# Rows for the next projections turned by VectorE and through memory instead of by TensorE, and the first six weight loads issued at once

## The chip, the core and the metric

The kernel runs on one core of a Trainium2 chip. The core has TensorE (PE in the profile, for matrix products), VectorE (DVE), ScalarE (ACT), GpSimd (POOL) and SyncE (SP), which issues the transfers. Each engine takes its instructions in order, and semaphores join the queues. The metric is the device time of one execution in microseconds, lower is better; every kernel is run several times and the median is given.

## The reference

A block of attention and an MLP over x of 16 x 256 rows of width 256, with a layer norm before and after each part and a residual around it:

```
x = x + layernorm(attention(layernorm(x)))     # 16 heads of 128, causal, biases on q, k, v, o
x = x + layernorm(mlp(layernorm(x)))           # 2048 wide, out = (gelu(gate) * up) @ Wd.T

scores = where(causal, q @ k.T / sqrt(128), -1e5);  attn = softmax(scores)
W = LUT[4-bit codes] * scales[block of 32]     # gate, up and down weights of the MLP
```

All of it is fp32. The layer norms have no weights: (x - mean) / sqrt(var + 1e-5).

## The kernel before

**Precision.** TensorE multiplies in fp32r, so each operand is split into a high part (`_hi`, rounded by a copy on ScalarE) and a low part (`_lo`, the difference, on VectorE or GpSimd), and a product is three matmuls, hi x hi, lo x hi and hi x lo (`three`, lines 700 to 702).

**Tiling.** The 4096 rows are eight chunks (`NCH`) of 512 rows: two sequences, four tiles of 128 rows (`TT`). The width of 256 is two tiles for the contraction (`KT`), and these take every second column, kt, kt+2, and so on. Attention is 128 steps, n = 16 c + j for chunk c and head j; the MLP after it is eight chunks of sixteen tiles of its hidden width. `xnT` holds the normalised rows of a chunk, turned (width on the partitions, 512 rows along), in a high and a low part; all projections of a chunk read it.

**One step of attention.** `step_plan(n)` is written out by hand: projections q and k of head n+1, T(n) (VectorE turns the probabilities of head n in blocks of 32 x 32 into `turned`), out(n-3), z(n-2), pT(n-1), scores(n+1). In steps with n % 4 = 1 the four value tiles of the next four heads, v0 to v3, follow. In step 14 of a chunk, before, the plan also holds xT 0 and xT 1: TensorE transposes the next chunk's normalised rows out of `stream`, four 128 x 128 transposes for each (line 719), ScalarE and VectorE evict them into `xnT_hi` and `xnT_lo`. Projections, z and xT take the three PSUM banks `fbank` in turns, and a bank is free once the low part of what it held is written. Scores use three banks `ubank`.

**VectorE's order** is that of the plan with z moved behind the scores. Then follow, at the place "sum", the reciprocals of the softmax sums (line 901) and what `extra(c, j, "sum")` adds, and after v3, at "end", what `extra(c, j, "end")` adds. Two tables say what is added: `X1_AT`, the parts of the norm and residual of the attention's output of the chunk before (`finish_x1`), and `NEXT_AT`, the parts of the next chunk's layer norm (`norm_next_x`: 0 and 1 statistics, 2 their aggregates, 3 and 4 standardising). GpSimd takes the square roots in between, in steps `X1_ROOTS` and `NEXT_ROOTS`. `spread` unpacks 4-bit weights of the MLP beside all this.

**The probabilities' way through memory.** A turn in blocks of 32 leaves the blocks in the wrong partitions. In each step SyncE stores `turned` to a scratch in memory (`send`, line 488) and, once stored, loads it back in four pieces, each to its 32 partitions (`fetch`, line 498), into `back`, whence ScalarE takes pT. SyncE's queue (`load_program`) holds per step: send, the loads of weights (`load_pair`, chunk 0 only), fetch, store and load of the MLP's unpacked weights, and then, by j, a half of the next x (j = 3, 5), a half of x1's store (11, 13) or a half of the residual's x (15 and the next 1). `load_pair` uses two buffers (`raw`, `RAW` = 2) in turns: pair n waits until pair n-2 is split.

**The MLP.** `mlp_plan(c, j)`: gate and up products of tile j+2, then the down product of tile j. `finish_y` (j < 6) and `norm_next_y` (j = 7 to 10) add the norms on VectorE (`between`). At j = 13, before, the next chunk's rows are transposed on TensorE into `gbank` and `hbank` and evicted into `xnT`.

## Time and profile before

| | |
|---|---|
| median of 3 runs | 1584.81 us (1583.91 to 1586.49) |
| profiled execution | 1591.08 us, span 1588.4 us, granted clock 0.998 |
| TensorE busy | 1561.3 us, 98% |
| VectorE | 1061.5 us, 67% |
| ScalarE | 974.1 us, 61% |
| GpSimd | 712.5 us, 45% |
| transposes of rows, TensorE | 64 in attention, 56 in the MLP |
| traffic | 167.69 MB, mean 106 GB/s |

The span is the time on the engines and the profiled execution's own time is a little longer. Busy shares are averages over the whole span. A matmul of 512 columns is listed with 0.39 us, but a new one starts every 0.23 us, since they are pipelined; lengths of stretches are therefore read as the distance of two starts. I cut attention at the first scores matmul of each step (line 724).

### The profile page before, as it was taken

To read this page: it belongs to the slowest core of one execution; us is meant where nothing else is said; L and a number is where in the kernel's file an instruction comes from. 1 tells how busy PE (TensorE), PEld (TensorE's weight loads), DVE (VectorE), ACT (ScalarE), POOL (GpSimd) and SP (SyncE) were. 2 spreads that over 40 slices of the span, in tenths; PEclk is the share of its full clock that TensorE was granted. 3 is DMA by queue.
4 is the path that set the end of the run, shared out by engine and by line. 5 is a ranking of instruction groups with operands and counts; after the bars stand their busy time and mean duration, and the time that the engine had idled before them with its cause. 6 is when DMAs were issued, how large, how long until landed. Compare 5 with 4: busy or idle time off the path is not lost.

```text
span 1588.4 us, 28430 instructions
## 1 busy us (share of the span) xinstructions
PE 1561.3 (98%) x9600; PEld 1397.9 (88%) x9600; DVE 1061.5 (67%) x3074; ACT 974.1 (61%) x2433; POOL 712.5 (45%) x1069
## 2 busy tenths in 40 slices
PE   7999999999999999999999999999999999999998
PEld 5889898988998899889899989898888888888887
DVE  4656677677677777777767766666656565565665
ACT  5887677667776676767776767644444444444443
POOL 4674454545554455444554544333333333333333
PEclk9999999999999999999999999999999999999999
DMA  4554434443444344444443454471000011000000
GB/s 118 178 174 122 140 116 139 149 138 124 143 148 138 123 144 131 140 130 131 149 143 117 142 163 136 155 278 41 27 14 27 14 32 36 14 28 14 27 14 27
DMA packets 157440, 167.69 MB, mean 106 GB/s; under 512 B 15856, under 2 KB 130672, under 8 KB 157296
## 3 DMA queue, kind: packets, MB, share of 16 engines
q1 hardware_dynamic: 157296, 165.89, 32.9%
q8 instruction: 76, 1.25, 0.3%
q14 instruction: 68, 0.56, 0.1%
HBM read 94.53 MB, written 71.30 MB: 104 GB/s over the span
## 4 chain that ended last, share of the span: by engine, by line
PE 79%; DMA 6%; ACT 6%; DVE 5%; SPq 3%; issue 1%; POOL 1%; DVEq 0%; POOLq 0%
PE fbank L700 13%; PE fbank L701 13%; PE fbank L702 13%; PE obank L702 6%; PE obank L701 6%; PE obank L700 6%; PE ubank L700 5%; PE ubank L702 5%; PE ubank L701 5%; DMA turned_scratch<-turned 3%; PE ubank L724 3%; PE fbank L802 2%; DMA back<-turned_scratch 2%; SPq L498 2%; ACT probs L597 1%
## 5 line engine op out<-in xcount | busy, mean ns | idle before, releaser
L700 PE MATMUL fbank<-xnT_hi,wqk_hi 128*128 128x512 f32 x768 | 302.9, 394 | 3.7 <-POOL wqk_lo L1215 2.7
L701 PE MATMUL fbank<-xnT_lo,wqk_hi 128*128 128x512 f32 x768 | 301.3, 392 | 0.0
L702 PE MATMUL fbank<-xnT_hi,wqk_lo 128*128 128x512 f32 x768 | 300.7, 392 | 0.0
L1246 POOL TENSOR_TENSOR pT_lo<-back,pT_hi 128x512 fp32r<-128x512 f32 x128 | 166.1, 1298 | 274.3 <-ACT pT_hi L662 274.3
L608 ACT ACTIVATE w_raw<-fbank 128x512 f32<-128x512 f32 x128 | 76.5, 598 | 254.3 <-PE fbank L702 254.3
L1208 POOL TENSOR_SCALAR probs<-probs,rsum 128x128 f32<-128x128 f32 (+1 forms) x512 | 209.2, 428 | 20.7 <-DVE rsum L901 17.7
L702 PEld LDWEIGHTS fbank<-xnT_hi,wqk_lo 128*128 128x128 f32 x768 | 145.1, 189 | 31.8
L893 DVE CUSTOM_DVE_ANT_0 probs<-ubank,mask 128x128 f32<-128x128 f32 (+1 forms) x512 | 154.9, 355 | 26.4 <-PE ubank L702 26.1
L700 PEld LDWEIGHTS fbank<-xnT_hi,wqk_hi 128*128 128x128 f32 x768 | 145.2, 189 | 27.6 <-issue 2.9
L701 PEld LDWEIGHTS fbank<-xnT_lo,wqk_hi 128*128 128x128 f32 x768 | 145.3, 189 | 22.5
L982 DVE SCALAR_TENSOR_TENSOR w_raw<-w_raw,fbank 128x512 f32<-128x512 f32 x128 | 88.0, 687 | 104.0 <-ACT w_raw L608 102.2
L1226 POOL TENSOR_TENSOR kT_lo<-probs,kT_hi 128x512 fp32r<-128x512 f32 x64 | 83.1, 1298 | 160.4 <-ACT kT_hi L617 160.4
L988 DVE SCALAR_TENSOR_TENSOR probs<-w_raw,fbank 128x512 f32<-128x512 f32 x128 | 88.1, 688 | 97.8 <-ACT w_raw L612 97.8
L1226 POOL TENSOR_TENSOR v_lo<-probs,v_hi 128x512 fp32r<-128x512 f32 x64 | 82.8, 1294 | 153.4 <-ACT v_hi L617 153.4
L578 ACT ACTIVATE zT_hi<-fbank,bias_v 128x512 fp32r<-128x512 f32 x128 | 87.4, 683 | 104.0 <-PE fbank L802 104.0
L700 PE MATMUL obank<-wo_hi,zT_hi 128*128 128x256 f32 x512 | 143.5, 280 | 0.0
L702 PE MATMUL obank<-wo_hi,zT_lo 128*128 128x256 f32 x512 | 143.4, 280 | 0.0
L701 PE MATMUL obank<-wo_lo,zT_hi 128*128 128x256 f32 x512 | 142.9, 279 | 0.0
L880 DVE SCALAR_TENSOR_TENSOR kT_lo<-fbank,bias_k,kT_hi 128x512 fp32r<-128x512 f32 x128 | 95.8, 749 | 54.4 <-ACT k_early L589 54.0
L1051 DVE STREAM_TRANSPOSE turned<-probs 128x384 f32<-128x384 f32 x256 | 131.5, 552 | 0.0
L597 ACT ACTIVATE probs<-probs,nmax 128x256 f32<-128x256 f32 x256 | 126.8, 495 | 0.0
L595 ACT ACTIVATE probs<-probs,nmax 128x128 f32<-128x128 f32 x256 | 100.7, 393 | 18.2 <-DVE nmax L893 15.6
(124 smaller groups left out, 4566.1 us busy)
## 6 DMA issues: line engine op xcount, KB each, us to landing
turned_scratch<-turned SPq DMA_DIRECT2D x128, 384.0 KB, 2.6
back<-turned_scratch SPq DMA_DIRECT2D x512, 96.0 KB, 2.2
w_raw<-in_w_pairs SPq DMA_DIRECT2D x32, 256.0 KB, 3.3
w_hi_scratch<-w_hi SPq DMA_DIRECT2D x48, 128.0 KB, 2.0
w_lo_scratch<-w SPq DMA_DIRECT2D x48, 128.0 KB, 2.0
x_res<-in_x SPq DMA_DIRECT2D x16, 256.0 KB, 2.9
wqk_hi<-w_hi_scratch SPq DMA_DIRECT2D x16, 256.0 KB, 4.6
wqk_lo<-w_lo_scratch SPq DMA_DIRECT2D x16, 256.0 KB, 5.0
```

The costliest lines, as they stand in the source:

```text
L595: act.activation(pr[:, 0:P], pr[:, 0:P], ACT.Exp, bias=nmax[:, 0:1], scale=-1.0, accum_out=sums[:, 0:1])
L597: act.activation(pr[:, P:384], pr[:, P:384], ACT.Exp, bias=nmax[:, 1:2], scale=-1.0, accum_out=sums[:, 1:2]).then_inc(s.exp, 1)
L700: nc.tensor.matmul(out, a[0], b[0], start=start, stop=False, skip_group_check=skip)
L701: nc.tensor.matmul(out, a[0], b[1], start=False, stop=False, skip_group_check=skip)
L702: return nc.tensor.matmul(out, a[1], b[0], start=False, stop=stop, skip_group_check=skip)
L880: ins = dve.scalar_tensor_tensor(dst, bank, bias, hi.bitcast(F32), ALU.add, ALU.subtract)
L893: last = dve.tensor_tensor_reduce(out=pr[:, lo:hi], in0=bank[:, lo:hi], in1=mask, scale=-SCALE, scalar=3.0e38, op0=ALU.add, op1=ALU.min, a ...
L988: after(dve.scalar_tensor_tensor(act_v, mem.th[j % 2], 1.0, mem.gbank[slot(n)][:], ALU.add, ALU.mult))
L1051: dve.transpose(mem.turned[:, :, :, b, :].rearrange("p k u j -> p u k j"), mem.probs[b].rearrange("p (u k j) -> p u k j", u=3, k=4)).then_ ...
L1208: last = pool.tensor_scalar(pr[:, lo:hi], pr[:, lo:hi], mem.rsum[i][:, at:at + 1], 1.0, ALU.mult, ALU.mult)
L1226: pool.tensor_tensor(lo, mem.act_v[j % 2], hi.bitcast(F32), ALU.subtract).then_inc(s.iT_lo, 1)
L1246: pool.tensor_tensor(lo[:].rearrange("p u b (a j) -> p (u b) a j", j=32), mem.back[m % 2][:, :, 0:2].rearrange("p a u b j -> p (u b) a j") ...
```

## The change

**Attention.** The plan's xT entries go. In step 9, at "sum", VectorE turns the four standardised row tiles of the next chunk in blocks of 32 x 32 (`turn_rows`); the source is read with a stride of two columns, since a contraction tile takes every second column. SyncE stores the 512 KB to a new scratch and loads them back in four pieces into `x_in`, behind step 9's fetch. In step 14, behind k, an entry "rows" stands for two copies on ScalarE (`rows_hi`) and two differences on VectorE (`rows_lo`) into `xnT`. The next chunk's layer norm moves forward, statistics to step 1, roots to step 3, standardising to step 5 (in place, in `x_in`); the loads of x that feed it move to step 15 of the chunk before, both halves. The residual's loads go to steps 1 and 3, and two parts of `finish_x1` from step 9 to steps 10 and 12.

**MLP.** The next rows are normalised at j = 7 and 8 and turned at j = 8, go through memory likewise, and are split at j = 12, into `xnT` or, in every second chunk, into `zT` and `pT`, which the MLP has free.

**Weights.** `FIRST_PAIRS` is 6: six loads go at once, into `raw`, `x_res` and `back`; every later one comes a step sooner.

```diff
-FIRST_PAIRS = 4
+FIRST_PAIRS = 6
-X1_ROOTS, NEXT_ROOTS = 6, 13
+X1_ROOTS, NEXT_ROOTS = 6, 3
 def step_plan(n):
     plan = [("q", n + 1), ("k", n + 1), ("T", n)]
     if n % HEADS == HEADS - 2:
-        plan += [("xT", 0)]
+        plan.insert(2, ("rows", n // HEADS + 1))
     if n > 2:
         plan += [("out", n - 3)]
-    if n % HEADS == HEADS - 2:
-        plan += [("xT", 1)]
 def mlp_plan(c, j):
-    if j == NT - 3:
-        return ahead + ([("xT", 0)] if c < NCH - 1 else []) + [("down", j)]
+    if j == NT - 4 and c < NCH - 1:
+        return ahead + [("rows", c + 1), ("down", j)]
 def load_program(...):
     def load_pair(n):
-        if n >= RAW:
-            sp.wait_ge(s.w_split, n - RAW + 1)
-        sp.dma_start(mem.raw[:, n % RAW], w_pairs[n]).then_inc(s.w[n % RAW], 16)
+        if n < FIRST_PAIRS:
+            sp.dma_start(mem.raw_of(n), w_pairs[n]).then_inc(s.first_w[n], 16)
+        else:
+            sp.wait_ge(s.w_split, n - RAW + 1 if n >= FIRST_PAIRS + RAW else RAW)
+            sp.dma_start(mem.raw_of(n), w_pairs[n]).then_inc(s.w[n % RAW], 16)
+    def send_rows(n):
+        sp.wait_ge(s.rows_turned, 2 * n + 2)
+        if n:
+            sp.wait_ge(s.rows_back, 64 * n)
+        sp.dma_start(rows_v.rearrange("a i k c -> (a i) k c"),
+                     mem.turned_at(n).rearrange("p k t r i -> p k (t r i)")
+                     ).then_inc(s.rows_sent, 16)
+    def fetch_rows(n):
+        sp.wait_ge(s.rows_sent, 16 * (n + 1))
+        for k in range(4):
+            sp.dma_start(mem.rows_back[32 * k:32 * k + 32].rearrange("p a t r i -> p a (t r i)"),
+                         rows_v[:, :, k].rearrange("a i c -> i a c")).then_inc(s.rows_back, 16)
         fetch(n)
+        if j == 9:
+            send_rows(c)
+            fetch_rows(c)
-        if j in (3, 5):
-            next_x(c, (j - 3) // 2)
-        elif c and j in (11, 13):
+        if c and j in (11, 13):
             store_x1(c, (j - 11) // 2)
         elif j == 15:
-            load_res(c, 0)
-            if c == NCH - 1:
-                load_res(c, 1)
-        elif c and j == 1:
-            load_res(c - 1, 1)
+            for i in range(2):
+                if c < NCH - 1:
+                    next_x(c + 1, i)
+                else:
+                    load_res(c, i)
+        elif c and j in (1, 3):
+            load_res(c - 1, (j - 1) // 2)
 def scalar_program(...):
+    def rows_hi(n, dst):
+        act.wait_ge(s.rows_back, 64 * (n + 1))
+        for kt in range(KT):
+            act.activation(dst[0][kt].rearrange("p (t a i) -> p t a i", a=4, i=BLK),
+                           mem.rows_back[:, :, :, kt, :].rearrange("p a t i -> p t a i"),
+                           ACT.Copy).then_inc(s.rows_hi, 1)
 def vector_program(...):
+    def turn_rows(n, t):
+        for i in (t, t + 1):
+            last = dve.transpose(mem.turned_at(n)[:, :, i].rearrange("p k r i -> p r k i"),
+                                 x_in[:, i, :].rearrange("p (k j r) -> p r k j", r=KT, j=BLK))
+        last.then_inc(s.rows_turned, 1)
+    def rows_lo(n, dst):
+        for kt in range(KT):
+            dve.wait_ge(s.rows_hi, KT * n + kt + 1)
+            dve.tensor_tensor(dst[1][kt].rearrange("p (t a i) -> p t a i", a=4, i=BLK),
+                              mem.rows_back[:, :, :, kt, :].rearrange("p a t i -> p t a i"),
+                              dst[0][kt].bitcast(F32).rearrange("p (t a i) -> p t a i", a=4, i=BLK),
+                              ALU.subtract).then_inc(s.rows_lo, 1)
-    X1_AT = {(5, "end"): (0, 1, 2), (9, "end"): (3, 4, 5, 6)}
-    NEXT_AT = {(10, "sum"): (0,), (12, "sum"): (1, 2), (13, "end"): (3, 4)}
+    X1_AT = {(5, "end"): (0, 1, 2), (9, "end"): (3, 4), (10, "sum"): (5,), (12, "sum"): (6,)}
+    NEXT_AT = {(1, "end"): (0, 1, 2), (5, "end"): (3, 4), (9, "sum"): (5, 6)}
     def between(c, j):
-        elif 7 <= j < 11 and c < NCH - 1:
-            norm_next_y(j - 7, c)
+        elif j == 7 and c < NCH - 1:
+            for part in range(2):
+                norm_next_y(part, c)
+        elif j == 8 and c < NCH - 1:
+            for part in range(2, 5):
+                norm_next_y(part, c)
```

VectorE's queue in step 9 of chunk 3, from the reciprocals on, before:

```order
913 L901 RECIPROCAL rsum<-sums 128x2 x2
914 L878 TENSOR_TENSOR v_lo<-fbank,v_hi 128x512 x2
915 L916 TENSOR_SCALAR stream<-stream,mv,rstd 128x256 x4
916 L932 TENSOR_TENSOR stream<-stream,x_res 128x512 x2
917 L956 TENSOR_SCALAR spread<-words 128x128
918 L958 SCALAR_TENSOR_TENSOR spread<-words,spread 128x128
```

and after (`w_raw<-x_in` are the turned rows, written to the weights' former buffer):

```order
918 L943 RECIPROCAL rsum<-sums 128x2 x2
919 L964 STREAM_TRANSPOSE w_raw<-x_in 128x2x4x32 x4
920 L920 TENSOR_TENSOR v_lo<-fbank,v_hi 128x512 x2
921 L958 TENSOR_SCALAR stream<-stream,mv,rstd 128x256 x4
922 L1014 TENSOR_SCALAR spread<-words 128x128
923 L1016 SCALAR_TENSOR_TENSOR spread<-words,spread 128x128
```

Four turns of 128 x 256 stand ahead of the value tiles' low parts, and the two residual sums (L932 before) have left.

VectorE's queue where step 14 of chunk 3 goes over into step 15, before:

```order
989 L880 SCALAR_TENSOR_TENSOR qT_lo<-fbank,bias_q,qT_hi 128x256
990 L880 SCALAR_TENSOR_TENSOR kT_lo<-fbank,bias_k,kT_hi 128x512
991 L1051 STREAM_TRANSPOSE turned<-probs 128x3x4x32 x2
992 L878 TENSOR_TENSOR xnT_lo<-fbank,xnT_hi 128x512 x2
993 L893 ISA probs,nmax<-ubank,mask 128x128
```

and after:

```order
992 L922 SCALAR_TENSOR_TENSOR qT_lo<-fbank,bias_q,qT_hi 128x256
993 L922 SCALAR_TENSOR_TENSOR kT_lo<-fbank,bias_k,kT_hi 128x512
994 L971 TENSOR_TENSOR xnT_lo<-x_in,xnT_hi 128x512 x2
995 L1109 STREAM_TRANSPOSE turned<-probs 128x3x4x32 x2
996 L935 ISA probs,nmax<-ubank,mask 128x128
```

The rows' low parts have moved ahead of the turn of the probabilities, and their source is `x_in` instead of a PSUM bank.

SyncE's queue in steps 15 and 16 (chunk 3 into 4), before:

```order
262 L498 DMA back<-turned_scratch 32x4x192 x4
263 L468 DMA x_res<-in_x 128x2x256
264 L488 DMA turned_scratch<-turned 128x768
265 L498 DMA back<-turned_scratch 32x4x192 x4
266 L480 DMA w_hi_scratch<-w_hi 128x256
```

and after:

```order
267 L527 DMA back<-turned_scratch 32x4x192 x4
268 L486 DMA x_in<-in_x 128x2x256 x2
269 L517 DMA turned_scratch<-turned 128x768
270 L527 DMA back<-turned_scratch 32x4x192 x4
271 L509 DMA w_hi_scratch<-w_hi 128x256
```

Two loads of the next x now stand between the fetch of one step's probabilities and the send of the next's, where one load of the residual stood.

VectorE's queue in step 1 of chunk 0, before:

```order
35 L901 RECIPROCAL rsum<-sums 128x2 [waits exp_ready] x2
36 L880 SCALAR_TENSOR_TENSOR qT_lo<-fbank,bias_q,qT_hi 128x256 [waits full_hi]
37 L880 SCALAR_TENSOR_TENSOR kT_lo<-fbank,bias_k,kT_hi 128x512 [waits full_hi]
38 L878 TENSOR_TENSOR v_lo<-fbank,v_hi 128x512 [waits full_hi]
39 L1051 STREAM_TRANSPOSE turned<-probs 128x3x4x32 [waits turned_stored,probs_ready]
40 L1051 STREAM_TRANSPOSE turned<-probs 128x3x4x32 [waits probs_ready]
```

and after:

```order
37 L922 SCALAR_TENSOR_TENSOR kT_lo<-fbank,bias_k,kT_hi 128x512 [waits full_hi]
38 L920 TENSOR_TENSOR v_lo<-fbank,v_hi 128x512 [waits full_hi]
39 L948 BN_STATS stats<-x_in 128x6 [waits x_loaded]
40 L948 BN_STATS stats<-x_in 128x6
41 L948 BN_STATS stats<-x_in 128x6 [waits x_loaded,dve_chain]
42 L948 BN_STATS stats<-x_in 128x6
43 L953 BN_AGGR mv<-stats 128x2 [waits dve_chain]
44 L953 BN_AGGR mv<-stats 128x2 x3
45 L1109 STREAM_TRANSPOSE turned<-probs 128x3x4x32 [waits turned_stored,probs_ready]
46 L1109 STREAM_TRANSPOSE turned<-probs 128x3x4x32 [waits probs_ready]
```

The statistics of the next rows stand behind the last value tile and ahead of the turn of the probabilities.

## Rows read from the trace of the kernel before

**Rows 1.** the head of the page: span, then busy time of each engine

```profile
span 1588.4 us, 28430 instructions
PE 1561.3 (98%) x9600; PEld 1397.9 (88%) x9600; DVE 1061.5 (67%) x3074; ACT 974.1 (61%) x2433; POOL 712.5 (45%) x1069
```

**Rows 2.** waits of TensorE: waiter, releaser, total us, times, longest

```profile
PE ubank L724 <- DVE kT_lo L880: 4.4, 8, 1.4
PE fbank L700 <- POOL wqk_lo L1215: 2.7, 1, 2.7
PE fbank L700 <- DVE v_lo L878: 1.8, 4, 0.6
```

**Rows 3.** window of step 9, chunk 3: stretch, length, busy by engine, clock, DMA

```profile
476.47:488.36 11.89, 11.89 (x70) 10.47 (x69) 8.87 (x28) 7.25 (x18) 3.94 (x8) 1.00 0.27 87
```

**Rows 4.** windows, scores of step 14 to those of step 15, their sum

```profile
sum 107.23, PE 104.78 PEld 91.33 DVE 70.20 ACT 66.97 POOL 38.17; mean PE 13.10 PEld 11.42 DVE 8.78 ACT 8.37 POOL 4.77
```

**Rows 5.** windows of step 1, chunks 1 to 7: the first, and the sum

```profile
157.25:170.08 12.83, 12.23 (x70) 10.40 (x69) 6.87 (x23) 7.31 (x19) 4.81 (x9) 1.00 0.37 111
sum 85.51, PE 84.29 PEld 73.20 DVE 47.12 ACT 52.04 POOL 31.86; mean PE 12.04 PEld 10.46 DVE 6.73 ACT 7.43 POOL 4.55
```

**Rows 6.** windows in the MLP: a quiet tile, and a chunk's sixteen

```profile
1300.25:1304.39 4.14, 4.14 (x27) 3.66 (x26) 2.06 (x4) 1.75 (x3) 1.29 (x1) 1.00 0.00 0
1239.88:1307.13 67.25, 67.25 (x394) 59.58 (x393) 41.32 (x77) 30.14 (x52) 23.06 (x20) 1.00 0.08 24
```

**Rows 7.** timeline of VectorE, step 9, chunk 3: start, length, what, idle before

```profile
475.86 1.03 DVE L1051 STREAM_TRANSPOSE turned<-probs 128x384 f32<-128x384 f32 x2
...
479.82 0.17 DVE L901 RECIPROCAL rsum<-sums 128x2 f32<-128x2 f32 x1 [0.62 <-ACT probs L597]
480.31 0.69 DVE L878 TENSOR_TENSOR v_lo<-fbank,v_hi 128x512 fp32r<-128x512 f32 x1 [0.32 <-ACT v_hi L577]
...
483.16 1.50 DVE L916 TENSOR_SCALAR stream<-stream,mv,rstd 128x256 f32<-128x256 f32 x4
```

**Rows 8.** timeline of TensorE, the fourth value tile of step 9, chunk 3

```profile
481.72 0.39 PE L700 MATMUL fbank<-wv_hi,xnT_hi 128*128 128x512 f32 x1
```

**Rows 9.** timelines of VectorE and TensorE, step 9, chunk 0

```profile
98.10 0.69 DVE L878 TENSOR_TENSOR v_lo<-fbank,v_hi 128x512 fp32r<-128x512 f32 x1 [0.32 <-ACT v_hi L577]
98.85 0.50 PE L700 MATMUL fbank<-wv_hi,xnT_hi 128*128 128x512 f32 x1 [0.54 <-DVE v_lo L878]
```

**Rows 10.** timelines of VectorE and TensorE, step 5, chunk 3

```profile
451.90 1.53 DVE L906 BATCH_NORM_STATS2 stats<-stream 128x6 f32<-128x256 f32 x4
453.47 0.38 DVE L911 BATCH_NORM_AGGREGATE mv<-stats 128x2 f32<-128x6 f32 x4
...
455.83 0.75 DVE L880 SCALAR_TENSOR_TENSOR kT_lo<-fbank,bias_k,kT_hi 128x512 fp32r<-128x512 f32 x1 [0.43 <-ACT k_early L589]
457.11 0.39 PE L724 MATMUL ubank<-k_early,q_early 128*128 128x128 f32 x2
```

**Rows 11.** timelines of VectorE and ScalarE, step 14 into 15, chunk 3

```profile
522.01 1.29 DVE L878 TENSOR_TENSOR xnT_lo<-fbank,xnT_hi 128x512 fp32r<-128x512 f32 x2 [0.32 <-ACT xnT_hi L577]
523.88 0.40 ACT L595 ACTIVATE probs<-probs,nmax 128x128 f32<-128x128 f32 x1 [0.21 <-DVE nmax L893]
```

**Rows 12.** timeline of SyncE, steps 0 and 1 of chunks 1 and 4

```profile
150.23 0.42 SPq L468 DMA_DIRECT2D x_res<-in_x  x1
151.25 0.33 SPq L488 DMA_DIRECT2D turned_scratch<-turned  x1
156.16 1.75 SPq L498 DMA_DIRECT2D back<-turned_scratch  x4
...
536.20 0.34 SPq L488 DMA_DIRECT2D turned_scratch<-turned  x1
538.80 1.74 SPq L498 DMA_DIRECT2D back<-turned_scratch  x4
```

**Rows 13.** timeline of TensorE, the scores of step 3

```profile
39.57 0.49 PE L724 MATMUL ubank<-k_early,q_early 128*128 128x128 f32 x2 [1.44 <-DVE kT_lo L880]
```

More of the change, by code:

```diff
@@ L657, in scalar_program @@
                 full(count, mem.zT[0][:], bank, mem.bias_v[:, h:h + 1]).then_inc(s.hi, 1)
-            else:
-                full(count, mem.xnT[0][:, m, :], bank).then_inc(s.hi, 1)
+        elif kind == "rows":
+            rows_hi(m - 1, mem.rows[0])
         elif kind == "pT":
@@ L715, in project @@
         last.then_inc(s.full, 1)
-    def transpose_x(src, kt, bank):
-        for t in range(TT):
-            last = nc.tensor.transpose(bank[:, t * P:(t + 1) * P], src[:, t, kt:D:KT], mem.ident[:])
-        return last
     def scores(u, i, b):
@@ L1043, in vector_program @@
                     extra(c, j, "sum")
-            else:
-                full(count, mem.xnT[1][:, m, :], mem.xnT[0][:, m, :], bank)
+        elif kind == "rows":
+            rows_lo(m - 1, mem.rows[0])
         elif kind == "T":
```

138 lines of the change are left out of this document (77 added, 61 removed).

## The prediction

> **What bounds the kernel now.** I read the page's head first: TensorE is busy for 98% of a span of 1588.4 us [rows 1], so only two things can move the time: work taken off TensorE, and waits put on it or taken from it. The view of what TensorE waited for came next [rows 2]. Three of its lines matter here: 4.4 us for VectorE's low part of the keys before scores (eight times, the longest 1.4), 2.7 us once, at the start, for the low part of a head pair's weights, and 1.8 us for a value tile's low part (four times). Then I cut the span at the first scores matmul of each step and looked at the windows between two cuts. A step with four value tiles takes 11.89 us where nothing is late [rows 3], and that is my yardstick for steps 1, 5, 9 and 13. A step that exceeds its yardstick contains foreign work or a wait. Last I took the timelines of VectorE, ScalarE and SyncE in the steps that the change touches. VectorE is busy for 67% of the span [rows 1], yet in those steps its queue, in order, decides.
>
> The profiled execution took 1591.08 us and the median is 1584.81, so the former is 6.3 above. All terms below are differences. They are summed against the profiled execution, and the sum is then applied to the median.
>
> **What leaves TensorE, attention.** The eight windows from the scores of step 14 to those of step 15 sum to 107.23 us [rows 4]. They hold step 13's values, so the yardstick is 8 x 11.89 = 95.12. The excess, **12.1 us**, is the transposes, their eviction through the three banks (two more places in the round) and the wait for the rows. The change takes all of it: step 14 has no transpose, no extra bank and no wait for fresh rows, since the rows went out in step 9, five steps earlier. The trip is a 512 KB store and four loads of 128 KB; the like trip of the probabilities, 384 KB, is stored and its fetch issued 2.60 us after the send [rows 12]. Even three times 2.60 for each way is far less than the more than 25 us from step 9 to 14. I cost the trip at nothing; its cover is this distance.
>
> **What leaves TensorE, MLP.** A quiet tile takes 4.14 us, and the sixteen tiles of one chunk, with its eight transposes, 67.25 [rows 6]. 67.25 - 16 x 4.14 = 1.01 us; seven chunks have them: **7.1 us**. VectorE is busy for 2.06 of a tile's 4.14 us, so two parts of the row norm and the four turns, put into tile 8 (some 3.0 us at the prices of [rows 7]), make it late by about 2.2 us for one tile and hold nobody up, since products are consumed two tiles later. I take nothing for it; its ends are 0 and the uncovered 1 us per chunk, 7.
>
> **The start.** TensorE's 2.7 us [rows 2] are the wait for the low part of the third head pair, whose load waits today until the first buffer is split. With six loads at once this wait goes. But VectorE now computes the statistics of the next rows (1.53 and 0.38, sum 1.9 us, the prices of step 5 in [rows 10]) in step 1, ahead of the turn of the probabilities, so what follows that turn (exponentials, and the next keys' low part) comes later. Scores 3 start at 39.57 now, after a wait of 1.44 us for the keys' low part [rows 13]. Without the statistics they would start at 39.57 - 2.3; with them nearly all of it is given back, and I get 39.2 or so. **-0.3 us**, ends -2.3 and +1.
>
> **What the turn adds in step 9.** No row turns a normalised row. The nearest is the turn of probabilities: two instructions of 128 x 384 take 1.03 us, 1.34 ns a column [rows 7]. Four turns of 256 columns are 1.37 to 1.50 us (the upper end is the standardising of four tiles of 128 x 256 in the same place); I take 1.43. They stand between the reciprocal and the first value tile's low part. The reciprocal ends at 479.99; the turns end at 481.42; the low part at 482.1. The fourth value tile needs this bank and starts at 481.72 now [rows 8], so it would start at about 482.2: **0.5 us** in seven chunks. In chunk 0 there is no slack: the reciprocal ends at 97.78, low part and fourth tile follow at once, and the tile waits already [rows 9]; the turns end at 99.2, the low part at 99.85 and the tile starts at 99.95 instead of 98.85: 1.1 us. Together **+4.6**. The ends are 0 (the turn costs less than 0.9 us) and, at twice the price, 13.2.
>
> By these rows the turn on VectorE costs the path 4.6 us and saves 19.2. The Trainium skill ("VectorE: DVE Perf Modes", The three transpose paths and Rules for kernel authors) speaks against the exchange: it gives TensorE 390 ns and VectorE 311 ns for a 128 x 128 transpose, the latter in 32 x 32 blocks only, and advises TensorE where the result may go to PSUM. By its 390 ns, as an estimate, the 120 removed transposes would be worth 46.8 us; the windows above say 19.2, and I go by them.
>
> **What moves on VectorE.** Step 5 gets the standardising of the next rows ahead of the low parts of queries and keys. That is four instructions, 1.50 us [rows 7]. VectorE idles 0.43 us before the keys' low part, which ends at 456.58, and scores start at 457.11 [rows 10]. 1.50 - 0.43 - 0.53 = 0.54 us; chunks 1 to 6 have a full step 5: **+3.2**. In chunk 0 the statistics of the attention's output are absent, in chunk 7 the unpacking of the MLP's weights, each over 1 us, and I count nothing there. The ends are 0 and 1.07 x 7 = 7.5. In step 14 the rows' low part (1.29 us) moves ahead of the turn of probabilities. Scores start at 522.26, as the cuts say, the low part ends at 523.2 and the exponentials start 1.62 us after the scores [rows 11]. With low part and turn both behind the keys, which end about as the scores start, the mask begins 0.9 us later than now, 1.85 us after the scores, and the exponentials at 2.5. These, and with them the next step's queries and keys on ScalarE, come 0.88 later; about 0.5 of slack as in [rows 10] leaves 0.4 us: x 7 = **+2.8**, ends 0 and 6.2. The residual sums that leave step 9 go to steps 10 and 12, where they stand beside work of TensorE.
>
> **What moves on SyncE.** Both loads of the next x now stand at step 15, after its fetch and directly ahead of the send of step 16's probabilities. The trace has one load of 256 KB in this place: with it the send at 151.25 is fetched at 156.16, after 4.91 us; a quiet one, at 536.20, after 2.60 [rows 12]. The step with the slow send took 12.83 us instead of 11.89 [rows 5]. Two such loads hold at least as much: 7 x 0.94 = 6.6 us. Now these seven steps lose 85.51 - 7 x 11.89 = 2.3 us [rows 5], so the net is **+4.3**. Ends: 0, should the loads have landed before the send matters, and twice the price less 2.3, +10.9.
>
> **Sum.** -12.1 - 7.1 - 0.3 + 4.6 + 3.2 + 2.8 + 4.3 = **-4.6 us**. 1591.08 becomes 1586.5, and the median 1584.8 becomes **1580.2**.
>
> **Rivals.** *B, the added waits are mostly hidden.* VectorE is idle for 3.0 of the 11.89 us of a value step [rows 3], and each wait that I added is a few tenths, the difference of large numbers. If none comes, the time is 1584.8 - 19.5 = 1565.3; with half of them 1572.8. Against it: the queue is in order, and the present waits for the same producers [rows 2] show that the slack is used up in places.
>
> *C, the turn of rows runs at half rate.* The source is every second column, the source of the probabilities' turn is dense. At 0.62 us a turn instead of 0.36, four are 2.5 us, and the fourth value tile is late by 1.05 us more, eight times: +8.4, **1588.6**, slower than before. It decides from (1588.0 - 1580.2) / 8 / 4 = 0.24 us more per turn, 0.6 us each. For it: no row has a stride on VectorE's turn. Against it: TensorE's transposes read with the same stride, and the other row instructions take their time per column.
>
> The Trainium skill ("SBUF — State Buffer", Specifications) says that lines of 16 bytes run at full rate with two hits each, which a stride of two in fp32 has. By that rule C would not occur; no run here shows it.
>
> *D, only the start fails or the boundary costs double.* The six loads share the queues and the first pair comes later: +1 instead of -0.3; or two loads hold the send longer than one. This gives 1581.5 to 1587. It is also the case in which the trip's 13 MB of further traffic slows the probabilities' trips.
>
> **How the numbers follow.** My own case, with each size off by a third, is 1577 to 1584: chance 0.45, of which 0.27 lies below 1581.6 and 0.18 above. B has 0.33 and is faster. C has 0.10. D has 0.12: 0.10 within the bound and 0.02 beyond. A measurement of this kernel tells about 0.2%, 3.2 us, from no change: faster means below 1581.6, slower above 1588.0. Faster 0.27 + 0.33 = 0.60, same 0.28, slower 0.12. The range from 1570 to 1588 leaves out the best third of B (0.10) and most of C (0.10).
>
> **What would show it.** Right: no transpose row on TensorE outside the start; the windows from step 14 to 15 fall to 11.9 to 12.5 us and the MLP's chunk to 66.3. Four turns at 0.34 to 0.38 us each, and a wait of TensorE for the value's low part, some 0.5 us eight times. A wait for the keys' low part in step 5 of about 0.5 us, and value steps 1 of every chunk at 12.8. Wrong: turns above 0.6 us (C), value steps 1 and 5 at 11.89 (B), sends that take over 5 us to come back in the middle of a chunk (D), or a wait of TensorE for the rows' low part in step 14, which would say that the trip is not hidden.

## The result and the profile after

The change makes the kernel slower: a median of 1591.6 us (1589.49 to 1591.92, 5 runs) against 1584.7 (5 runs), a ratio of 1.0040 with a 95% interval of 1.0029 to 1.0051. Measured a second time, the same kernel has 1.0045 (1.0032 to 1.0058). I had forecast 1580.2, and slower with a chance of 0.12.

The two profiled executions do not show this by their spans. The head of the page of the kernel after:

```profile
span 1587.3 us, 28341 instructions
PE 1555.9 (98%) x9480; PEld 1384.5 (87%) x9480; DVE 1083.9 (68%) x3134; ACT 974.1 (61%) x2433; POOL 718.0 (45%) x1069
```

The span is 1.1 us shorter than in [rows 1]. The trace before is of an execution of 1591.08 us, above all five of its timed runs (highest 1586.49), the one after of the fastest of five; a second trace of the kernel before has a span of 1579.9. Spans of one kernel differ by 8.5 us, though all engines have the same durations. What differs is waiting: ScalarE waits 18.3 us for the probabilities' trips in the first trace and 14.9 in the second, and 9.7 and 7.1 us for the weights of chunk 0. So a difference of 7 us must be read from stretches in which nothing is late, or from several traces. TensorE has lost 120 transposes and 5.4 us of busy time. What it waits for (waiter, releaser, total us, times, longest):

```profile
PE ubank L775 <- DVE kT_lo L922: 8.2, 16, 2.5
PE fbank L756 <- DVE v_lo L920: 4.1, 6, 1.1
```

Beside [rows 2]: the wait for weights at the start is gone, the waits for the keys' low part have doubled in number and nearly in time, and the value tiles' have more than doubled.

The same cuts as in [rows 4], scores of step 14 to those of step 15, eight chunks; then steps 1 and 5, chunks 1 to 7 (sums of busy time and means follow the sum of lengths), and step 9 of chunk 3:

```profile
sum 95.42, PE 95.41 PEld 84.09 DVE 52.57 ACT 67.38 POOL 34.79; mean PE 11.93 PEld 10.51 DVE 6.57 ACT 8.42 POOL 4.35
sum 87.61, PE 85.11 PEld 73.34 DVE 61.37 ACT 51.05 POOL 30.60; mean PE 12.16 PEld 10.48 DVE 8.77 ACT 7.29 POOL 4.37
sum 86.76, PE 84.41 PEld 73.17 DVE 65.44 ACT 50.44 POOL 27.37; mean PE 12.06 PEld 10.45 DVE 9.35 ACT 7.21 POOL 3.91
477.64:489.89 12.25, 12.19 (x70) 10.40 (x69) 9.35 (x31) 7.60 (x19) 4.85 (x9) 1.00 0.58 179
```

The transposes' step is at its yardstick (95.1). Step 1 holds 4.4 us above 83.2, step 5 3.5 us, step 9 0.36 us in this chunk. So far that is near what I had worked out. Two things are not. First, the MLP. Eight tiles in a row, before, then after in a chunk whose rows lie in `zT` and `pT`, then after in a chunk that reads `xnT`:

```profile
1128.48:1161.60 33.12, 33.12 (x194) 29.31 (x193) 21.00 (x41) 14.00 (x24) 12.12 (x11) 1.00 0.11 32
```
```profile
1128.45:1162.16 33.71, 33.71 (x195) 29.30 (x193) 22.91 (x47) 14.07 (x24) 11.46 (x11) 1.00 0.14 48
1203.91:1237.03 33.12, 33.12 (x195) 29.32 (x193) 22.07 (x43) 14.67 (x26) 11.55 (x10) 1.00 0.21 64
```

TensorE is busy without a gap in all three, at full clock, with the same matmuls; in `zT` and `pT` a tile takes 4.21 us instead of 4.14. Four chunks have it. From the last scores to the end the kernel before takes 555.4 us, both traces of the changed kernel 553.8, and two kernels below, whose rows lie elsewhere, 549.7 and 549.6: so the place costs **4.2 us** (64 tiles at 0.073 would be 4.7), and without it the MLP's part gains 5.7. Second, the ordinary steps behind the one that I priced. I took four traces of the old layout of attention (the two of the kernel before, and two of experiments below that leave chunks 1 to 7 of attention as they were) and four of the new (two of the changed kernel, two of experiments that only move tensors in SBUF), cut all of them alike, and summed each step over chunks 1 to 7 (so many windows as there are):

| window, scores to scores | old, mean | new, mean | difference | my term |
|---|---|---|---|---|
| step 14 | 93.2 | 83.7 | -9.5 | -11.1 |
| step 15 | 39.2 | 41.0 | +1.8 | +2.8 |
| step 0 | 45.2 | 47.7 | **+2.5** | none |
| step 1 | 45.3 | 47.8 | **+2.5** | none |
| step 1 with its values | 84.8 | 88.2 | +3.4 | +4.3 |
| step 5 with its values | 83.5 | 86.7 | +3.2 | +3.2 |
| the step behind it | 45.1 | 45.8 | +0.6 | none |
| step 9 with its values | 83.4 | 86.6 | +3.2 | +3.5 |
| step 12 | 45.9 | 46.9 | +1.0 | none |
| all others | 320.2 | 319.3 | -1.0 | none |
| chunk 0, all | 126.0 | 126.0 | 0.0 | -0.2 |

(The values of step 1 stand in the window from scores 2 to scores 3, and so on. For chunk 0 my term is -1.0 for the transposes, -0.3 for the start and +1.1 for the turn. One of the four old traces has six first loads, so the old mean of chunk 0 is of the other three; they spread from 123.6 to 128.0.) The sum is +7.8 us where I had +2.5 for attention. The terms that I priced for chunks 1 to 7 come out within 1.6 us each; 5.6 us are in windows in which I had priced nothing.

### The profile page after: what moved, and what is told of

It is laid out like the page before. It is cut to its first block, busy times and chain, and to the rows that moved or that the text cites. A ratio compares the mean times of both kernels' runs of the same rounds, so it can differ in the third digit from the quotient of the medians.

```text
span 1587.3 us, 28341 instructions
## 1 busy us (share of the span) xinstructions
PE 1555.9 (98%) x9480; PEld 1384.5 (87%) x9480; DVE 1083.9 (68%) x3134; ACT 974.1 (61%) x2433; POOL 718.0 (45%) x1069
## 4 chain that ended last, share of the span: by engine, by line
PE 71%; DMA 8%; ACT 8%; DVE 8%; SPq 3%; issue 2%; POOL 0%; DVEq 0%
PE fbank L756 12%; PE fbank L757 11%; PE fbank L758 11%; PE obank L756 6%; PE obank L758 6%; PE obank L757 6%; PE ubank L758 5%; PE ubank L756 5%; PE ubank L757 5%; DMA turned_scratch<-turned 5%; DMA back<-turned_scratch 3%; PE ubank L775 2%; ACT probs L645 2%; SPq L527 2%; ACT probs L643 2%
## 5 line engine op out<-in xcount | busy, mean ns | idle before, releaser
L756 PE MATMUL fbank<-xnT_hi,wqk_hi 128*128 128x512 f32 x640 | 252.0, 394 | 1.1 <-DVE xnT_lo L920 1.1
L757 PE MATMUL fbank<-xnT_lo,wqk_hi 128*128 128x512 f32 x640 | 251.2, 393 | 0.0
L758 PE MATMUL fbank<-xnT_hi,wqk_lo 128*128 128x512 f32 x640 | 250.8, 392 | 0.0
L1273 POOL TENSOR_SCALAR probs<-probs,rsum 128x128 f32<-128x128 f32 (+1 forms) x512 | 215.1, 438 | 26.9 <-DVE rsum L943 24.6
L1040 DVE SCALAR_TENSOR_TENSOR w_raw<-w_raw,fbank 128x512 f32<-128x512 f32 x128 | 87.5, 683 | 93.2 <-ACT w_raw L656 92.1
L758 PEld LDWEIGHTS fbank<-xnT_hi,wqk_lo 128*128 128x128 f32 x640 | 120.8, 189 | 26.2
L756 PEld LDWEIGHTS fbank<-xnT_hi,wqk_hi 128*128 128x128 f32 x640 | 121.2, 189 | 21.4 <-DVE xnT_lo L920 1.5
L757 PEld LDWEIGHTS fbank<-xnT_lo,wqk_hi 128*128 128x128 f32 x640 | 121.0, 189 | 19.7
## 6 DMA issues: line engine op xcount, KB each, us to landing
x_in<-rows_scratch SPq DMA_DIRECT2D x60, 128.0 KB, 2.8
w_hi_scratch<-w_hi SPq DMA_DIRECT2D x48, 128.0 KB, 2.0
w_lo_scratch<-w SPq DMA_DIRECT2D x48, 128.0 KB, 2.0
```

Source lines behind the costliest of these rows:

```text
L756: nc.tensor.matmul(out, a[0], b[0], start=start, stop=False, skip_group_check=skip)
L757: nc.tensor.matmul(out, a[0], b[1], start=False, stop=False, skip_group_check=skip)
L758: return nc.tensor.matmul(out, a[1], b[0], start=False, stop=stop, skip_group_check=skip)
L1273: last = pool.tensor_scalar(pr[:, lo:hi], pr[:, lo:hi], mem.rsum[i][:, at:at + 1], 1.0, ALU.mult, ALU.mult)
```

## Experiments

All edits are against the changed kernel unless said otherwise, and all ratios are to the kernel before, measured beside it. The changed kernel itself has 1.0045 (1.0032 to 1.0058); it was measured beside the kernels of the first four expectations only, and the others are held against that figure. A ratio within about 0.0018 of it does not tell a kernel from the changed one by itself, and there the size rests on the windows of single traces.

**Two traces more: the kernel before and the changed kernel, unchanged.**

> The kernel before, unchanged, for a second trace. The first one was of an execution that took 1591.08 us by itself, 6.4 above the median of 1584.7. Theory 'the sum was made against a trace with more waits than usual': the new profiled execution takes about 1585, and the windows from the scores of step 14 to those of step 15 sum to 103 to 105 us instead of 107.23, steps 1 to 1.5 us less than 85.51. Rival 'the profile itself costs 6 us': it takes 1591 again with the same windows. Ratio to before 1.000.

Ratio 1.0004 (0.9994 to 1.0014). The windows of step 14 in this trace:

```profile
sum 105.51, PE 104.38 PEld 91.43 DVE 69.90 ACT 67.74 POOL 38.07; mean PE 13.05 PEld 11.43 DVE 8.74 ACT 8.47 POOL 4.76
```

105.5 instead of 107.2, and 8.5 us less in the span. So the trace on which the sum rested had more waits than usual. The mean of the four old traces is 106.2, and the term of 12.1 us was about 1 us too large for that reason.

> The changed kernel, unchanged. Its profiled execution was the fastest of five (1589.49 against a median of 1591.6). Theory: a typical execution has 2 us more waits in the steps at a chunk's start (0 to 2), where the loads of x stand before the sends; MLP tiles that read zT and pT take 4.21 us again. Ratio 1.003 to 1.005.

Ratio 1.0045, span 1589.9, `zT` and `pT` at 4.21 again. From the first scores to the last it takes 1.5 us more than in this kernel's first trace, 0.7 of it in steps 0 to 2: half the theory's 2 us, and not there alone.

**Where the MLP's rows lie.** First both tensors beside `xnT`, low in SBUF (new lines only; the old ones go):

```diff
         self.xnT = [sb(f"xnT_{s}", [P, KT, CHUNK], F32R) for s in ("hi", "lo")]
+        self.pT = [sb(f"pT_{s}", [P, 2, 2, P], F32R) for s in ("hi", "lo")]
+        self.zT = [sb(f"zT_{s}", [P, CHUNK], F32R) for s in ("hi", "lo")]
```

> The changed kernel with pT and zT allocated beside xnT, low in SBUF, nothing else changed. In the changed kernel the MLP chunks 1, 3, 5, 7, whose rows lie in zT and pT, take 4.21 us a tile, the others 4.14; 64 tiles, 4.5 to 4.8 us in all. Theory 'the place in SBUF': tiles fall to 4.14 in all chunks, and the time is 4.5 to 5 us under the changed kernel's, about 1587. Rival 'two tensors of 512 columns instead of one, or the work in those chunks': 4.21 remains and the time stays at 1591 to 1592.

Ratio 1.0023 (1.0014 to 1.0032). Eight tiles in the chunk that had 33.71:

```profile
1126.76:1159.88 33.12, 33.12 (x194) 29.31 (x193) 21.91 (x47) 14.00 (x24) 11.42 (x12) 1.00 0.11 32
```

The opposite, in the kernel before: `xnT` allocated last.

> The kernel before with xnT allocated last, high in SBUF behind zT, nothing else changed. Theory 'the place in SBUF': each matmul of 512 columns that reads xnT as its moving operand takes 233 instead of 227 ns, which makes MLP tiles 4.21 us in all eight chunks (128 x 0.07 = 9 us) and, for queries and keys, twelve matmuls in each of 128 steps (128 x 12 x 6.5 ns = 10 us): 1603 us. In the value tiles xnT is the stationary operand, and I expect nothing there. Rival: 1585, tiles at 4.14.

Ratio 1.0080 (1.0066 to 1.0094), 13 us. Eight tiles; the next chunk's take 33.70:

```profile
1128.88:1162.59 33.71, 33.71 (x195) 29.33 (x194) 21.83 (x45) 13.99 (x24) 12.24 (x12) 1.00 0.11 32
```

All chunks are now slow in a kernel that has nothing of the change. The place is the cause, not the two tensors. Attention lost too: an ordinary step takes 6.51 instead of 6.45 us, a value step 12.04 instead of 11.89. The latter is more than I had expected, because there `xnT` is the stationary operand and `wv`, low in SBUF, the moving one, and it loses as well. For queries and keys I had expected 0.08 us a step and it is 0.06, and the whole is 13 us where I had forecast 18. Then qT and pT as the second place, `zT` left where it was (an excerpt; the old lines of `qT` and `pT` go, and `pT` stands behind `xnT` as in the first experiment):

```diff
+        queries = sb("qT", [P, 4, 2, P], F32R)          # beside xnT, with pT
+        self.qT = [[queries[:, 2 * s + i] for s in range(2)] for i in range(2)]
-                     [[p[:] for p in self.zT],
+                     [[queries[:, 2 * s:2 * s + 2].rearrange("p i b q -> p (i b q)") for s in range(2)],
```

> The changed kernel; the odd MLP chunks' rows lie in qT and pT, both allocated beside xnT, and zT stays where it was. With pT and zT moved, the MLP tiles fell to 4.14 us, but an ordinary attention step rose from 6.45 to 6.47 us, and the products that read zT as stationary operand took 118 to 120 ns instead of 117 to 118. Theory 'a matmul is slower when its two operands lie far apart in SBUF': MLP 4.14 in all chunks; scores (qT low, kT high) may lose what z loses, a step is 6.45 to 6.50; 4 us under the changed kernel, ratio to before 1.002. Rival 'only the moving operand's place counts': steps at 6.45 but for z, 5 us under.

Ratio 1.0022 (1.0013 to 1.0032); MLP tiles at 4.14 everywhere, an ordinary step at 6.44. The products of the output projection read `zT` as stationary and `wo`, which lies between, as moving operand (ns of one are the last number ahead of the bar). With `zT` low (first experiment), and with `zT` high (this one):

```profile
L758 PE MATMUL obank<-wo_hi,zT_lo 128*128 128x256 f32 x512 | 144.9, 283 | 0.0
```
```profile
L760 PE MATMUL obank<-wo_hi,zT_lo 128*128 128x256 f32 x512 | 143.3, 280 | 0.0
```

So low is not simply better. "A pair is faster where its two operands lie near each other" fits these products and the MLP's, but not the products of `pT` (moving) with the values `v` (stationary, high). In the changed kernel both lie high and one takes 281 ns. In the first experiment and in this one `pT` stands low, at the same place:

```profile
L757 PE MATMUL fbank<-pT_lo,v_hi 128*128 128x256 f32 x256 | 70.7, 276 | 0.0
```
```profile
L759 PE MATMUL fbank<-pT_lo,v_hi 128*128 128x256 f32 x256 | 71.8, 280 | 0.0
```

Far apart it is faster in one and the same in the other. Queries and keys do not fit either: in both kernels 8 KB more stand between `xnT` and its weights, and their twelve matmuls in a step take 2.75 us in the first, 2.72 in this one and 2.735 before (medians, from start to start). That the place decides is shown, for the MLP in both directions; by which rule is open.

**The low parts of step 14 behind the turn.**

```diff
     if n % HEADS == HEADS - 2:
-        plan.insert(2, ("rows", n // HEADS + 1))
+        plan.insert(3, ("rows", n // HEADS + 1))
```

> The changed kernel with the rows' low parts behind the turn of step 14's probabilities instead of ahead of it. Theory 'they delay the exponentials of step 15': the seven windows from the scores of step 15 to those of step 16 fall from 47.6 to 45.8 us, and the 0.1 to 0.2 us that the next step loses goes too: 2 to 3 us in all, 1591 where the changed kernel has 1593.9. Rival 'what is lost there comes from the transfers of x': no change.

Ratio 1.0024 (1.0014 to 1.0034), 3.3 us less than the changed kernel: the size was right, the way was not. Sums of the windows of step 15, step 0 and step 1, first after, then here:

```profile
sum 41.01, PE 39.99 PEld 35.85 DVE 31.14 ACT 29.36 POOL 17.55; mean PE 6.66 PEld 5.98 DVE 5.19 ACT 4.89 POOL 2.92
sum 47.11, PE 46.44 PEld 42.39 DVE 38.69 ACT 32.74 POOL 26.52; mean PE 6.63 PEld 6.06 DVE 5.53 ACT 4.68 POOL 3.79
sum 47.03, PE 46.15 PEld 42.27 DVE 31.15 ACT 35.82 POOL 25.71; mean PE 6.59 PEld 6.04 DVE 4.45 ACT 5.12 POOL 3.67
```
```profile
sum 42.80, PE 40.29 PEld 36.22 DVE 32.19 ACT 29.23 POOL 17.49; mean PE 6.71 PEld 6.04 DVE 5.37 ACT 4.87 POOL 2.92
sum 45.17, PE 45.17 PEld 41.81 DVE 36.51 ACT 34.15 POOL 27.79; mean PE 6.45 PEld 5.97 DVE 5.22 ACT 4.88 POOL 3.97
sum 45.18, PE 45.18 PEld 41.80 DVE 30.68 ACT 35.28 POOL 24.80; mean PE 6.45 PEld 5.97 DVE 4.38 ACT 5.04 POOL 3.54
```

Step 15 gets worse by 1.8 us, since TensorE now waits 0.4 us for the rows themselves; steps 0 and 1, in which I had priced nothing, lose their whole excess, and the step with step 1's values falls from 87.6 to 85.5 (86.4 and 86.7 in the two combinations below that contain this move). SyncE's queue shows why (chunk 3 into 4, the send of step 14, then the sends and fetches of steps 15 and 16, with the loads between), first after, then here:

```profile
523.08 0.34 SPq L517 DMA_DIRECT2D turned_scratch<-turned  x1
...
529.33 0.64 SPq L503 DMA_DIRECT2D scale<-in_scales  x1
530.07 0.40 SPq L517 DMA_DIRECT2D turned_scratch<-turned  x1
532.77 2.68 SPq L527 DMA_DIRECT2D back<-turned_scratch  x4
535.50 0.94 SPq L486 DMA_DIRECT2D x_in<-in_x  x2
536.54 0.42 SPq L517 DMA_DIRECT2D turned_scratch<-turned  x1
540.27 1.75 SPq L527 DMA_DIRECT2D back<-turned_scratch  x4
```
```profile
522.17 0.34 SPq L517 DMA_DIRECT2D turned_scratch<-turned  x1
...
527.78 0.64 SPq L503 DMA_DIRECT2D scale<-in_scales  x1
529.31 0.32 SPq L517 DMA_DIRECT2D turned_scratch<-turned  x1
531.67 2.45 SPq L527 DMA_DIRECT2D back<-turned_scratch  x4
534.16 0.95 SPq L486 DMA_DIRECT2D x_in<-in_x  x2
535.91 0.34 SPq L517 DMA_DIRECT2D turned_scratch<-turned  x1
539.14 1.75 SPq L527 DMA_DIRECT2D back<-turned_scratch  x4
```

After, step 14's send goes out 1.93 us behind the scores of step 15 (521.15), here 0.45 us behind them (521.72), and everything in the queue moves with it. Here the queue is empty for 0.9 and 0.8 us ahead of each later send, and the trips take 2.36 and 3.23 us. After, both sends go out 0.1 us after the transfer ahead of them and take 2.70 and 3.73. So the send is 1.5 us later behind the scores in step 14, and still 1.3 us later two steps on (1.93 against 0.59): the queue does not make it up in between. The removal shows that the late turn costs the excess of steps 0 and 1; that it does so by way of this queue is my reading of these rows.

**The loads of x in steps 14 and 15 instead of both in 15.**

```diff
+        elif c < NCH - 1 and j in (14, 15):
+            next_x(c + 1, j - 14)
         elif j == 15:
             for i in range(2):
-                if c < NCH - 1:
-                    next_x(c + 1, i)
-                else:
-                    load_res(c, i)
+                load_res(c, i)
```

> The changed kernel with the two loads of the next x in steps 14 and 15 instead of both in step 15. Theory 'two loads ahead of a send hold the probabilities': the eight windows of step 1 (scores 1 to 2) fall from 96.5 us to 93, those of step 0 and the one before by 0.5 to 1 each: 4 us under the changed kernel. Rival 'the residual's load in step 1 does it': step 1 stays at 96.5, the time too.

Ratio 1.0088 (1.0075 to 1.0102): 7 us worse, neither theory. (What the expectation calls 96.5 us are the windows that hold step 1's values, scores 2 to 3; they fell to 94.2.) The windows of step 1 itself, chunks 1 to 7, rose from 47.5 us to 54.0, and six of the seven are now 1.0 to 2.1 us above 6.45. Step 15's send goes out at once behind the moved load (0.10 us after it) and takes 3.7 us instead of 2.7. Two steps now have a load ahead of a send where one had two.

**The second load left out**, in chunks 1 to 7:

> The changed kernel without the second of the two loads of x in step 15 (chunks 1 to 7; their second half is left as it was, so the output is not the reference's). Theory 'what stands ahead of step 16's send costs': the windows of steps 0, and of step 1 after them, lose 4 us of their sum of 148 us, ratio 1.002. Rival 'the late turn of step 14 does it all, loads are free': ratio 1.0045.

Ratio 1.0037 (1.0025 to 1.0049). Step 1 with its values, in the second trace of the changed kernel, then here:

```profile
sum 87.46, PE 85.25 PEld 73.47 DVE 61.32 ACT 51.09 POOL 30.78; mean PE 12.18 PEld 10.50 DVE 8.76 ACT 7.30 POOL 4.40
```
```profile
sum 85.05, PE 84.34 PEld 73.62 DVE 60.95 ACT 51.59 POOL 29.90; mean PE 12.05 PEld 10.52 DVE 8.71 ACT 7.37 POOL 4.27
```

2.4 us there instead of 4 in all; steps 0 and 1 keep theirs (47.7 and 47.9). So what those two lose is not the second load's. What the step with the values loses is that load's in part, and in part the late turn's, since it fell to 85.5 without that. The ratios' intervals overlap, so the size rests on the windows, and in the four new traces of the table this sum lies between 87.1 and 90.7.

**The turns behind the value tiles.**

```diff
-    NEXT_AT = {(1, "end"): (0, 1, 2), (5, "end"): (3, 4), (9, "sum"): (5, 6)}
+    NEXT_AT = {(1, "end"): (0, 1, 2), (5, "end"): (3, 4), (9, "end"): (5, 6)}
```

> The changed kernel with the four turns behind step 9's value tiles, where the two residual sums stood before, instead of ahead of them. The sums took 1.29 us and the turns take 1.43, so the keys' low part should come 0.1 us later than before at most, and the value tiles' low parts on time. Theory 'the turns cost only by their place': the windows of step 9 fall from 99.3 us to 96.5, the value tiles' wait of TensorE goes; 2.5 us under the changed kernel. Rival 'VectorE has no room there either': the wait moves to the keys' low part and the windows stay within 0.5 us.

Ratio 1.0076 (1.0062 to 1.0091), 5 us worse. The window of step 9 in chunk 3, as expected, and those of step 12, chunks 3 and 7:

```profile
478.78:490.70 11.92, 11.92 (x70) 10.45 (x68) 8.90 (x30) 7.27 (x18) 3.83 (x8) 1.00 0.44 147
```
```profile
497.27:504.85 7.58, 6.62 (x46) 5.95 (x45) 5.23 (x20) 4.73 (x14) 3.86 (x8) 1.00 0.54 172
...
1012.83:1022.79 9.96, 7.08 (x47) 5.89 (x45) 4.42 (x16) 5.30 (x15) 2.87 (x5) 1.00 0.53 164
```

An ordinary step of 6.45 us takes up to 9.96. SyncE, in order, stood behind the rows' store, first after, then here (chunk 3):

```profile
486.80 1.73 SPq L541 DMA_DIRECT2D x_in<-rows_scratch  x4
490.35 0.34 SPq L517 DMA_DIRECT2D turned_scratch<-turned  x1
492.73 1.73 SPq L527 DMA_DIRECT2D back<-turned_scratch  x4
```
```profile
489.57 1.73 SPq L541 DMA_DIRECT2D x_in<-rows_scratch  x4
491.62 0.34 SPq L517 DMA_DIRECT2D turned_scratch<-turned  x1
494.71 2.99 SPq L527 DMA_DIRECT2D back<-turned_scratch  x4
```

The rows' loads end at 488.5 and the send follows 1.8 us later in the first case; in the second only 0.3 us, and its fetch comes after 3.1 us instead of 2.4. The turns' place ahead of the values, which costs 3.2 us, is what pays for the quiet in that queue.

**The same with the rows' loads a step later** (`fetch_rows` behind step 10's fetch):

> The changed kernel with the turns behind step 9's value tiles, as in a_turnend, and with the load of the turned rows moved on SyncE from step 9, where it stands ahead of step 10's send, behind the fetch of step 10. In a_turnend step 9 took 11.92 us, as the price of the place says, but SyncE stood behind the rows' store until the probabilities' send of step 10 came 1.9 us later, and the steps 12 lost 6 us in all. Theory 'SyncE's queue, in order, waits for the rows': step 9 stays at 11.92, the windows of step 12 fall from 59.3 to 53 us, and the time is 3 us under the changed kernel's. Rival 'the traffic itself delays the probabilities': step 12 stays above 56 us and the time at or above the changed kernel's.

Ratio 1.0097 (1.0083 to 1.0111). Step 9 stays at 11.92 and step 12 falls from 59.3 us to 56.3, but step 13 rises from 54.2 to 59.2 (all eight chunks). The rival holds: in both places tried the 512 KB delay the probabilities; unblocking the queue only moves the loss.

**The trip with a quarter of its data.**

> The changed kernel in which the turned rows of attention make the trip with a quarter of their data (one of four column blocks stored, one of four loads); the other three quarters of the rows are left as they were, so the output is not the reference's. Theory 'the rows' traffic in step 9 delays the next probabilities': step 12 of chunk 7 falls from 8.1 us to under 7, step 8 to 9 and 10 lose 0.5 less, 2 to 3 us in all, ratio 1.003. Rival 'the trip is free, as forecast': ratio 1.0045.

Ratio 1.0039 (1.0027 to 1.0051). Step 12 of chunk 7, after and here:

```profile
1007.48:1015.09 7.61, 6.62 (x47) 5.95 (x45) 3.93 (x15) 5.30 (x15) 2.90 (x5) 1.00 0.61 190
```
```profile
1009.72:1016.17 6.45, 6.45 (x46) 5.97 (x45) 4.30 (x16) 4.85 (x14) 2.95 (x5) 1.00 0.33 108
```

Against four traces with the whole trip this window is 1.2 to 2.0 us shorter; in it the MLP's weights are loaded. The store of the probabilities behind both was followed by its fetch after 5.27 and 5.57 us in the changed kernel's two traces and after 2.64 here. The other steps' sums lie within the spread of those four traces or at most 0.7 us outside it, either way. The ratio's interval holds both theories.

**The start.** The kernel before with six first loads, and the changed kernel with chunk 0's statistics in step 2:

> The kernel before with the six first loads at once, and nothing else of the change. Theory 'the six loads gain 2 to 3 us at the start, and the statistics in step 1 take it back': scores 4 start at 44 us or earlier where the kernel before has 44.6 and 46.8 in its two traces, ratio 0.9985. Rival 'the start is bound by something else': ratio 1.000 within 0.0005.

Ratio 0.9998 (0.9989 to 1.0007). From the first scores to the fifth it takes 26.1 us where the two traces before take 27.3 and 28.8, about 2 us. But the first scores come later in this trace, and scores 4 start at 45.1 us, between the 44.6 and 46.8 of the two traces before. So the gain on the whole is not shown; the ratio is that of the rival.

> The changed kernel with the statistics of the next rows in chunk 0 moved from step 1 (behind the value tiles, ahead of the turn) to step 2 (behind the reciprocals). Theory 'they hold back the turn of step 1': scores 3 start at 37 us instead of 38.8, and 1 to 2 us are gained. Rival 'they only move': scores 4 start at 47 us again and nothing is gained.

Ratio 1.0038 (1.0025 to 1.0052); first to fifth scores 26.8 us instead of 29.1 and 30.4 in the changed kernel's traces. So the statistics take back what the six loads give, by single traces; the ratio is not clear of the changed kernel's.

**Combinations.** Four moves, the two that failed among them:

> Four moves together: the MLP's rows in qT and pT low in SBUF (measured -3.6 us), the rows' low parts behind the turn in step 14 (-3.3), the turns behind step 9's values and the rows' load a step later (-3 expected). If they add up: 10 us under the changed kernel, ratio to before 0.998. If the last one brings nothing: 1.000.

Ratio 1.0042 (1.0030 to 1.0055), above both 0.998 and 1.000: the moved turns cost as much as the others bring. The three that help:

> The changed kernel with three moves together: MLP rows in qT and pT low in SBUF (ratio 1.0022 alone), the rows' low parts behind step 14's turn (1.0024 alone), chunk 0's statistics in step 2 (1.0038 alone); the changed kernel itself had 1.0045 then. If they add up: 0.9995. If the last two take the same wait away: 1.000 to 1.001.

Ratio 0.9995 (0.9986 to 1.0004), median 1584.3: they add up, to the kernel before and not beyond it. And the MLP's part alone, on the kernel before:

> The kernel before with the MLP's part of the change alone (rows turned by VectorE and through memory in the MLP, no transpose there), its alternate rows in qT and pT low in SBUF; attention as before, four first loads. Theory 'the MLP part gains and attention loses': a chunk of the MLP takes 70.55 us instead of 71.39, seven of them, 5.9 us; ratio to before 0.9963. Rival 'the trip costs in the MLP what the transposes cost': ratio 1.000.

Ratio **0.9966** (0.9955 to 0.9978), median 1579.7 against 1584.9: faster than both kernels. (The move of qT and pT comes with it, and an ordinary step of attention takes 6.44 instead of 6.45 us; but the MLP alone, from the last scores to the end, is 5.7 us shorter.) One chunk, before and here:

```profile
1262.99:1334.38 71.39, 71.39 (x418) 63.24 (x417) 43.95 (x82) 31.89 (x55) 24.94 (x22) 1.00 0.08 23
```
```profile
1251.08:1321.63 70.55, 70.55 (x410) 62.34 (x409) 45.27 (x86) 32.04 (x55) 24.41 (x21) 1.00 0.12 38
```

By subtraction from the kernel with qT and pT (1.0022, the same MLP), the attention and start parts of the change cost 0.56%, 8.9 us with some 2.4 us to either side, which agrees with the +7.8 of the table.

## Why the prediction was wrong

Two steps failed above all, and both are terms that the sum put at nothing. It followed the late turn of step 14 to the next scores and no further, where it costs some 5 us more in steps 0 and 1; and it gave no term to where the MLP's turned rows lie, which costs 4.2 us. In order of its steps:

- **What leaves TensorE, attention**, 12.1 us: 10.4 by the mean of four traces (9.5, and 0.9 in chunk 0). The step was right. About 1 us of its size came from one trace with more waits than usual, and 0.6 us are waits that the windows after still hold above the yardstick. With the MLP's 5.7 the 120 transposes were worth 16.1 us. The 390 ns that the Trainium skill gives for a transpose in bf16 ("VectorE: DVE Perf Modes", The three transpose paths), taken as an estimate for these in fp32, would have made it 46.8; the runs do not bear that out.
- **What leaves TensorE, MLP**, 7.1 us: 0.84 in an ordinary chunk, 5.7 us in all. The quiet tile as yardstick was right, but 17 tiles at 4.14 make 70.38, so 0.17 us of each chunk belongs to its end and not to the transposes. This part of the prediction failed at what it did not look at: where the turned rows lie. It has no term for the second place, `zT` and `pT`, and that place costs 4.2 us, most of the gain. No row before had shown these matmuls with their rows in another place.
- **The start**, -0.3: from the first to the fifth scores the changed kernel takes 29.1 and 30.4 us, and nine kernels above with the same start 28.8 to 29.6; the kernel before takes 27.3 and 28.8, and the one with the MLP's part alone 28.7. By the means that is +0.9, at my upper end of +1; the two pairs alone would say +1.7. The mechanism is the one that I had named.
- **The turn in step 9**, +4.6: +3.8. (Its upper end was reckoned wrongly: 1.43 us more in each of eight steps would be 16.0, not 13.2.) Four turns took 1.40 us where I had 1.43, and the value tile waits.

```profile
481.08 1.40 DVE L964 STREAM_TRANSPOSE w_raw<-x_in 128x256 f32<-128x256 f32 x4
482.41 0.65 DVE L920 TENSOR_TENSOR v_lo<-fbank,v_hi 128x512 fp32r<-128x512 f32 x1
```
```profile
483.11 0.50 PE L756 MATMUL fbank<-wv_hi,xnT_hi 128*128 128x512 f32 x1
```

  Rival C, half rate for the stride, is refuted by the first of these rows, 0.35 us a turn. By the rule on lines of 16 bytes in the Trainium skill ("SBUF — State Buffer", Specifications), a stride of two fp32 is free; this row agrees.
- **What moves on VectorE**, step 5, +3.2: +3.2, and 0.6 us in the step behind it that I had not counted. Step 14, +2.8: +1.8 in the step that I looked at. The exponentials start at 523.62, 2.47 us after the scores, where I had 2.5:

```profile
523.62 0.40 ACT L643 ACTIVATE probs<-probs,nmax 128x128 f32<-128x128 f32 x1 [1.07 <-DVE nmax L935]
```

  Here is the first step that failed. I followed the late turn from the mask through the exponentials to the next scores, on VectorE and ScalarE, and stopped there. The same turn is what SyncE's send waits for. Steps 0 and 1 lose 5.0 us by the table, and putting the low parts behind the turn takes all of it away (3.8 us in that trace). The prediction listed SyncE's queue for what was put into it, not for what comes late to it.
- **What moves on SyncE**, +4.3: +3.4; leaving out one of the two loads gives back 2.4.
- **The trip, costed at nothing** because five steps cover its length: its length is covered, its traffic is not. 1.2 to 2.0 us in chunk 7, and it is the reason why the turns did not come free in the other place. Rival D named this and got 0.12 with a time of at most 1587; it came true in part, and beside it stand the two steps above, which no rival named.

So the sum of -4.6 became +6.2 by the windows (+7.8 in attention, 1.6 less in the MLP), where the medians say +6.9. The 10.8 us between are 5.6 in windows behind those that I priced (the trip's among them), 4.2 for the place of the rows, 1.6 and 1.4 for gains that were sized too high, 0.2 in chunk 0, less 2.2 for losses that were (1.0, 0.9 and 0.3).

## What to carry to other kernels

When an instruction becomes late, follow every engine and queue that waits for it, the transfers' queue above all: an in-order queue with less slack per step than the lateness carries it on for several steps. A transfer costs by what is sent right behind it, and not only by its own length. When data moves to another buffer, compare the distance of two starts of the same matmul before and after, for the same instruction can cost another time there. And take a second trace of the kernel before, if terms of a few us are to be summed.

## What the runs showed of the hardware

A matmul of 512 columns in fp32r starts 227 ns after the one before it when both operands lie low in SBUF, and about 233 when the moving one lies high and the stationary one low, with TensorE busy without a gap at full granted clock. Over an MLP tile of twelve such matmuls it is 4.14 against 4.21 us. With the stationary operand high and the moving one low the value steps lost 0.09 us beyond the 0.06 us of their queries and keys. Neither height nor distance alone gives the rule: with `pT` low and `v` high a matmul was listed with 276 ns in one kernel and 280 in another. A store of 384 KB was followed by its fetch after 2.36 us where the queue had stood empty for 0.9 us, after 3.23 where it had for 0.8 us behind two loads of 256 KB, after 2.70 and 3.73 where it went out 0.1 us after the transfers ahead of it, and after 5.27 and 5.57 us in chunk 7, behind the rows' and the weights' loads. And two executions of one kernel differ by 8.5 us in span (1579.9 and 1588.4), with all engines at the same durations.
